# Projecting v in one matmul per tile with both weight parts side by side, and turning the row maxima with one matmul into 16 masked rows

## The reference

```python
# block 1: attention over the 1024 positions of an image, projections of width 32
q = einsum('mc,bcn->bmn', wq, x); k = ...wk...; v = ...wv...
att = softmax(einsum('bmi,bmj->bij', k, q), axis=2)
x = x + einsum('cm,bmn->bcn', wo, einsum('bij,bmj->bmi', att, v))
# block 2: tokens (1024 x 64 per image)
t = to_tokens(x)
u = layernorm(t);  t = t + softmax(u @ u.T) @ u
# block 3: 8 experts, the best 2 of each token
t = t + top2_mixture_of_experts(layernorm(t))
out = from_tokens(t)
```

## Time and profile before

| What | us |
|---|---|
| Median of 3 runs (237.2 to 237.84) | 237.38 |
| Time of the profiled execution | 236.11 |
| Its span, from first to last instruction | 234.4 |
| PE busy | 205.7 |
| DVE busy | 151.6 |
| ACT busy | 109.6 |
| POOL busy | 72.8 |

### The profile page before, as it was taken

The page is one execution under the profiler, slowest core; times in us unless marked ns, Lnnn a source line. Parts: engine busy times, 40 slices in busy tenths (PEclk is TensorE's granted clock), DMA queues, the critical chain, the costliest instruction groups (busy, mean ns, idle before and its releaser), DMA issues.

```text
span 234.4 us, 2786 instructions
## 1 busy us (share of the span) xinstructions
PE 205.7 (88%) x987; PEld 102.5 (44%) x987; DVE 151.6 (65%) x364; ACT 109.6 (47%) x170; POOL 72.8 (31%) x88
## 2 busy tenths in 40 slices
PE   6899899989997889899799999999999996682494
PEld 1545343735342435445345443543533433261382
DVE  2789666578159546846886787486835467999070
ACT  3533545575954552685345337664546751110101
POOL 8140000070403000110213577003776300874940
PEclk9999999999999999999999999999999999998578
DMA  3770000000000000000000000100000200000022
GB/s 101 137 166 15 3 0 0 0 1 3 1 0 0 3 0 0 0 0 3 0 1 0 3 1 9 35 0 3 0 0 0 49 0 0 0 0 0 0 48 45
DMA packets 3341, 3.67 MB, mean 16 GB/s; under 512 B 2176, under 2 KB 2432, under 8 KB 3328
## 3 DMA queue, kind: packets, MB, share of 16 engines
q1 hardware_dynamic: 3328, 3.50, 6.9%
HBM read 2.45 MB, written 1.05 MB: 15 GB/s over the span
## 4 chain that ended last, share of the span: by engine, by line
PE 62%; DVE 22%; ACT 6%; POOL 3%; issue 3%; DMA 1%; SPq 1%; DVEq 0%; POOLq 0%
PE acc L498 24%; DVE rowmax L1064 7%; PE ring L559 6%; PE ring L491 5%; PE ring L560 5%; PE ring L473 4%; PE ring L601 3%; PE ring L602 2%; DVE prod L1205 2%; DVE qst L1056 2%; DVE stats L1097 1%; ACT prob L870 1%; PE ring L535 1%; PE ring L462 1%; PE ring L583 1%
## 5 line engine op out<-in xcount | busy, mean ns | idle before, releaser
L873 ACT ACTIVATE prob<-ring,shift 128x1024 f32<-128x1024 f32 x32 | 35.6, 1113 | 36.6 <-PE ring L560 36.5
L1064 DVE TENSOR_REDUCE rowmax<-ring 128x1 f32<-128x1024 f32 x32 | 37.7, 1218 | 11.4 <-PE ring L473 11.3
L373 POOL TENSOR_TENSOR sm<-sm,minus_half 128x8 f32<-128x8 f32 x8 | 15.8, 1974 | 83.6 <-DVE sm L1107 83.6
L870 ACT ACTIVATE prob<-ring 128x1024 f32<-128x1024 f32 x32 | 32.0, 1026 | 16.7 <-PE ring L491 16.6
L498 PE MATMUL acc<-prob,val 128*64 128x512 f32 x128 | 31.1, 605 | 1.0 <-ACT prob L870 1.0
L498 PE MATMUL acc<-prob,u 128*64 128x512 f32 x128 | 31.2, 606 | 0.3 <-ACT prob L873 0.3
L559 PE MATMUL ring<-zst 128*128 128x512 f16 x64 | 24.5, 384 | 3.8 <-DVE rowmax L1064 2.7
L1205 DVE TENSOR_TENSOR prod<-ring,gate 128x1024 f32<-128x1024 f32 x16 | 19.3, 1219 | 12.0 <-PE ring L602 12.0
L473 PE MATMUL ring<-qst,kst 96*128 96x512 f32 x64 | 22.4, 436 | 2.3 <-DVE kst L1061 1.0
L560 PE MATMUL ring<-zsw,zst 128*128 128x512 f16 x64 | 24.3, 379 | 0.0
L491 PE MATMUL ring<-kst,qst 98*128 98x512 f32 x64 | 20.8, 423 | 3.0 <-DVE kst L1077 1.2
(11 more groups left out here) (152 smaller groups left out, 316.1 us busy)
## 6 DMA issues: line engine op xcount, KB each, us to landing
xin<-in_x SPq DMA_DIRECT2D x8, 256.0 KB, 4.0
out<-ob SPq DMA_DIRECT2D x6, 128.0 KB, 2.3
e_in<-in_L_ffn_expert_w SPq DMA_DIRECT2D x2, 128.0 KB
out<-ob SPq DMA_DIRECT2D x4, 64.0 KB, 2.0
eb_in<-in_L_ffn_expert_b SPq DMA_DIRECT2D x8, 2.0 KB
wo<-in_L_conv_wo SPq DMA_DIRECT2D x2, 8.0 KB, 2.2
r_in<-in_L_ffn_router_w SPq DMA_DIRECT2D x2, 2.0 KB
w<-in_L_conv_wq SPq DMA_DIRECT2D x1, 16.0 KB, 3.2
```

The costliest lines, as they stand in the source:

```text
L373: pool.tensor_tensor(sm[:, 3, :], sm[:, 2, :], minus_half[:, :], ALU.pow).then_inc(s_rs, 1)
L870: act.activation(prob1[:, j % DEEP, :], flat(filled(act, f"st{j}", b)), ACT.Exp).then_inc(s_p1, 1)
L873: act.activation(prob2[:, j % DEEP, :], flat(filled(act, f"s{j}", b)), ACT.Exp, bias=shift[:, :], accum_out=rsum2[b % 2][:, j:j + 1]).then ...
L1064: dve.tensor_reduce(rowmax[:, tile:tile + 1], flat(filled(dve, f"mx{tile}", b)), AX.X, ALU.max).then_inc(s_mx, 1)
```

## The change

**v and x.** The two weight tensors become one, `vx` of 128 columns: 32 for the high part of v's weights, 64 for x, 32 for the rest of v's weights. PE issues one matmul of 128 columns for each tile in place of two of 96. The two parts of v now lie side by side, so ACT copies the first into `vpart` and DVE adds the second to it (a new function `values` on DVE, a TENSOR_TENSOR of 128 x 256). The buffer is released by this DVE instruction (`s_v`), no longer by ACT.

**The maxima.** `nmax` holds the 8 high parts and the 8 rests of a position in 16 neighbouring columns, and one matmul turns them into 16 rows of 128. A DVE instruction (16 x 1024) spreads them: row r of `kst` gets its 128 numbers repeated 8 times, times a mask (`own_tile`) that is one only in the columns of its own tile. The second scores take 112 rows in place of 98, with 16 rows of ones in `qst`. ACT has no part in it any more.

```diff
@@ project_v @@
-                    o = (tile % 4) * (M + C)
-                    pe.matmul(buf[:, tile // 4, o:o + M + C], toks, vx1[:, :], start=True, stop=False)
-                    mm = pe.matmul(buf[:, tile // 4, o:o + M + C], toks, vx2[:, :], start=False, stop=True)
+                    o = (tile % 4) * P
+                    mm = pe.matmul(buf[:, tile // 4, o:o + P], toks, vx[:, :], start=True, stop=True)
@@ max_row on PE @@
-                for tile in range(T):
-                    c = col(tile)
-                    mm = pe.matmul(flat(buf)[0:ROW + 2, c:c + P], nmax[:, tile, :], ident_r[:, :], start=True, stop=True)
-                mm.then_inc(s_fill, 1)
+                pe.matmul(buf[0:ROW + 2 * T, 0, 0:P], nmax[:, :], ident_r[:, :], start=True, stop=True).then_inc(s_fill, 1)
@@ scores1 @@
-                    pe.wait_ge(s_mrow, 2 * (b + 1))
+                    pe.wait_ge(s_mrow, b + 1)
-                    mm = pe.matmul(buf[:, h, :], qst[home][0:ROW + 2, col(j):col(j) + P],
-                                   kst[home][0:ROW + 2, h * CHUNK:(h + 1) * CHUNK], start=True, stop=True)
+                    mm = pe.matmul(buf[:, h, :], qst[home][0:ROW + 2 * T, col(j):col(j) + P],
+                                   kst[home][0:ROW + 2 * T, h * CHUNK:(h + 1) * CHUNK], start=True, stop=True)
@@ release @@
-            table = {"w3": (s_wts, 3), "q": (s_qs, b + 2), "k": (s_ks, b + 2), "vx": (s_vx, 2 * b + 2),
-                     "mr": (s_mrow, 2 * b + 2), "po": (s_po, b + 1), "uT": (s_z, 2 * b + 2),
+            table = {"w3": (s_wts, 3), "q": (s_qs, b + 2), "k": (s_ks, b + 2), "vx": (s_v, b + 1),
+                     "mr": (s_mrow, b + 1), "po": (s_po, b + 1), "uT": (s_z, 2 * b + 2),
@@ ACT @@
-                act.activation(val[b % 2][:, :, 0:M].rearrange("p (a t) c -> p a t c", a=2), b4[:, :, :, 0:M],
-                               ACT.Copy).then_inc(s_vx, 1)
+                act.activation(vpart[:, :, :].rearrange("p (a t) c -> p a t c", a=2), b4[:, :, :, 0:M],
+                               ACT.Copy)
-            def max_row(b):
-                buf = filled(act, "mr", b)
-                act.activation(kst[b % 2][ROW:ROW + 2, 0:CHUNK], buf[ROW:ROW + 2, 0, :], ACT.Copy).then_inc(s_mrow, 1)
@@ DVE @@
+            def values(b):
+                buf, _ = PLACE[("vx", b)]
+                dve.wait_ge(s_vx, b + 1)
+                b4 = ring[:, buf].rearrange("p a (t c) -> p a t c", c=P)
+                dve.tensor_tensor(val[b % 2][:, :, 0:M].rearrange("p (a t) c -> p a t c", a=2), b4[:, :, :, M + C:P],
+                                  vpart[:, :, :].rearrange("p (a t) c -> p a t c", a=2), ALU.add).then_inc(s_v, 1)
             def max_row(b):
                 buf = filled(dve, "mr", b)
-                dve.tensor_copy(kst[b % 2][ROW:ROW + 2, CHUNK:N], buf[ROW:ROW + 2, 1, :]).then_inc(s_mrow, 1)
+                rows = slice(ROW, ROW + 2 * T)
+                shape = [2 * T, 2, T // 2, P]
+                mask = own_tile[rows, :].rearrange("r (g h) -> r h g", h=2)
+                dve.tensor_tensor(kst[b % 2][rows, :].rearrange("r (h g n) -> r h g n", h=2, n=P),
+                                  buf[rows, 0, 0:P].unsqueeze(1).unsqueeze(1).to_broadcast(shape),
+                                  mask.unsqueeze(3).to_broadcast(shape), ALU.mult).then_inc(s_mrow, 1)
@@ set-up on DVE @@
+            dve.tensor_tensor(own_tile[ROW:ROW + 2 * T, :], ident[ROW:ROW + 2 * T, ROW:ROW + T],
+                              ident[ROW:ROW + 2 * T, ROW + T:ROW + 2 * T], ALU.add)
-            dve.memset(vx2[:, M:M + C].bitcast(F32), 0.0)
```

More of the change, by code:

```diff
@@ L113, in build @@
         w2 = sb("w2", [P, 2, 3, M], F32R)
-        vx1 = sb("vx1", [P, M + C], F32R)
-        vx2 = sb("vx2", [P, M + C], F32R)
+        vx = sb("vx", [P, M + C + M], F32R)
         wo_blk = sb("wo_blk", [P, 2, C + 1])
@@ L145, in build @@
         rowmax = sb("rowmax", [P, T])
-        nmax = sb("nmax", [P, T, ROW + 2], F32R)
+        nmax = sb("nmax", [P, ROW + 2 * T], F32R)
+        own_tile = sb("own_tile", [P, T])
+        vpart = sb("vpart", [P, T, M])
         prob1 = sb("prob1", [P, DEEP, N])
@@ L210, in build @@
         s_ks = sem("k_split")
-        s_vx = sem("v_and_x_ready")
+        s_vx = sem("v_part_and_x_ready")
+        s_v = sem("v_ready")
         s_mx = sem("rowmax_ready")
@@ L346, in _ @@
                                pattern=[[-1, P]], channel_multiplier=1).then_inc(s_const, 1)
-            pool.memset(nmax[:, :, :].bitcast(F32), 0.0)
+            pool.memset(nmax[:, :].bitcast(F32), 0.0)
             for home in range(2):
@@ L351, in _ @@
             pool.wait_ge(s_pool, 3)
-            pool.memset(qst[0][ROW:ROW + 2, :].bitcast(F32), 1.0).then_inc(s_pool, 1)
+            pool.memset(qst[0][ROW:ROW + 2 * T, :].bitcast(F32), 1.0).then_inc(s_pool, 1)
             pool.wait_ge(s_pool, 4)
-            pool.memset(qst[1][ROW:ROW + 2, :].bitcast(F32), 1.0).then_inc(s_const, 1)
+            pool.memset(qst[1][ROW:ROW + 2 * T, :].bitcast(F32), 1.0).then_inc(s_const, 1)
             pool.wait_ge(s_const, 3)
@@ L503, in weigh1 @@
             def weigh1(b, j):
+                if j == 0:
+                    pe.wait_ge(s_v, b + 1)
                 if j == 0 and b:
@@ L928, in _ @@
                 act.activation(w1[:, :, r, :], buf[:, 0, 0:2 * M].rearrange("p (a m) -> p a m", a=2), ACT.Copy).then_inc(s_wr1, 1)
-            act.activation(vx1[:, 0:M], buf[:, 0, 2 * M:3 * M], ACT.Copy).then_inc(s_wr1, 1)
+            act.activation(vx[:, 0:M], buf[:, 0, 2 * M:3 * M], ACT.Copy).then_inc(s_wr1, 1)
             for name, dst, s_rounded in (("q", qst[0], s_qr), ("k", kst[0], s_kr)):
@@ L942, in _ @@
             round_k(1)
-            max_row(0)
             for j in range(4):
@@ L953, in _ @@
             values(1)
-            max_row(1)
             round_x(2)
@@ L1067, in negate_max @@
                 dve.wait_ge(s_mx, T * (b + 1))
-                hi = nmax[:, :, ROW:ROW + 1]
-                rm = rowmax[:, :].unsqueeze(2)
+                hi = nmax[:, ROW:ROW + T]
+                rm = rowmax[:, :]
                 dve.tensor_scalar(hi, rm, -1.0, None, ALU.mult).then_inc(s_nm, 1)
                 dve.wait_ge(s_nm, 2 * b + 1)
-                dve.scalar_tensor_tensor(out=nmax[:, :, ROW + 1:ROW + 2], in0=rm, scalar=-1.0, in1=hi.bitcast(F32),
+                dve.scalar_tensor_tensor(out=nmax[:, ROW + T:ROW + 2 * T], in0=rm, scalar=-1.0, in1=hi.bitcast(F32),
                                          op0=ALU.mult, op1=ALU.subtract).then_inc(s_nm, 1)
@@ L1088, in tokens1 @@
                 dve.wait_ge(s_po, b + 1)
-                dve.wait_ge(s_vx, 2 * b + 2)
+                dve.wait_ge(s_vx, b + 1)
                 dve.tensor_tensor(tok1[b % 2][:, :, :], tdiv[:, :, :], xt[b % 2][:, :, :], ALU.add).then_inc(s_tk1, 1)
@@ L1223, in _ @@
                               .to_broadcast([P, 2, 3, M]), w1[:, :, :, :].bitcast(F32), ALU.subtract).then_inc(s_wts, 1)
-            dve.memset(vx2[:, M:M + C].bitcast(F32), 0.0)
-            dve.tensor_tensor(vx2[:, 0:M], buf[:, 0, 2 * M:3 * M], vx1[:, 0:M].bitcast(F32), ALU.subtract).then_inc(s_wts, 1)
+            dve.tensor_tensor(vx[:, M + C:P], buf[:, 0, 2 * M:3 * M], vx[:, 0:M].bitcast(F32), ALU.subtract).then_inc(s_wts, 1)
             split_x0(1)
@@ L1234, in _ @@
                     dve.tensor_tensor(lo, ring[rows, k, h, :], lo.bitcast(F32), ALU.subtract).then_inc(s_split, 1)
-            for tile in range(T):
+            row_max(0, 0)
+            dve.wait_ge(s_const, 3)
+            values(0)
+            for tile in range(1, T):
                 row_max(0, tile)
@@ L1249, in _ @@
             negate_max(1)
+            values(1)
             dve.tensor_copy(ident_h[:, :], ident[:, :])
@@ L1257, in _ @@
             split_k(2)
+            values(2)
             dve.wait_ge(s_er, 2)
@@ L1281, in _ @@
             negate_max(2)
+            values(3)
             max_row(2)
```

5 lines of the change are left out of this document (2 added, 3 removed).

## The result

| | Before | After |
|---|---|---|
| Median, us (4 runs each, side by side) | 237.29 (237.08 to 237.84) | 240.79 (239.76 to 241.14) |
| Ratio, 95% interval | | 1.0129 [1.0103, 1.0155] |
| Profiled execution, us | 236.11 | 239.76 |
| Its span, us | 234.4 | 238.0 |
| Its mean granted TensorE clock | 0.974 | 0.960 |

The forecast was 236.6 us with a range up to 238.1. The last two rows of the table already point at what is missing from it: PE worked at a lower clock.

What follows compares the result with a forecast made beforehand. PE was taken as the bound in most places (62% of the chain), with hand-overs over DVE deciding at others. The terms summed to -0.76 us, giving 236.6 us against the median of 237.38, range 235.4 to 238.1.

Steps and rivals of the forecast that it cites:

- The terms of the sum: Image 0 +0.90, image 1 +0.16, image 2's v -0.64, image 3's v with image 2's maxima -1.01, image 3's maxima -0.10, start -0.07.
- PE waits for the spread at images 0 and 1: Ahead of the second scores: the spread adds 0.52 us at image 0; st0 of image 1 starts 0.38 later.
- taken: 0.114: Distance in us between starts of the new v matmuls, so each image's v costs PE 0.91 us less.
- 0.64 forecast: Image 2's v, inside image 1's scores: st6 waits for DVE, so 0.64 of PE's 0.91 us come through.
- The first exponential of image 1: Held by other ACT work before, it would follow st0 directly and start only 0.16 us later than before.
- V's 0.91 us less on PE buys nothing there: Image 0, first maxima tile: PE already waited 0.16 us for DVE's last split of k; image 0's term is +0.90.
- The 1.01 us that the prediction took off there: Image 3's v and image 2's maxima: DVE waited 2.57 us for PE, so st0 comes 1.01 us sooner.
- what could prove it wrong: A PE clock fall in the new 1.4 us pause before image 0's third maxima tile, for which it had no price.
- The spread was not dear: Rival: the spread costs more than 1.22 us, each extra d costing 4d, 238.2 us with d = 0.4; chance 0.14.
- DVE did not wait for POOL: Rival: `values(0)` is held until POOL's pass over x ends, +1.5, so 238.1 us; chance 0.06.
- v's matmuls gave back what they should: Rival: v matmuls start 0.2 us apart, an image's v gives back 0.22 us, total 237.7 us; chance 0.05.
- image 2's v gave its share: Rival: image 2's v gives nothing, as DVE is late to `values(2)` or st6 waits: -0.12, 237.3 us; chance 0.20.

Runs made afterwards that it cites:

- e8: The changed kernel unaltered, measured again beside e6 and e7 on one chip: 240.33 us (4 runs), ratio to before 1.0111.
- e7: The changed kernel with 6 more filler matmuls (read by nobody), in image 2's pauses only: 238.97 us (4 runs), ratio to before 0.9971.
- e14: As e13, with five more fillers in the pause ahead of image 1's second scores: 234.74 us (6 runs), ratio to before 0.9878.
- e13: As e1, with two more fillers before the first projections: 236.46 us (4 runs), ratio to before 0.99.
- e15: The same kernel as e13, measured again beside e14 on one chip: 236.78 us (11 runs), ratio to before 0.9957.
- e6: The changed kernel with 10 more filler matmuls, in image 0's pauses only: 238.56 us (4 runs).
- e5: The kernel before, without its 3 + 3 fillers around the turning of image 0's maxima: 239.91 us (10 runs), ratio to before 1.0048.
- e1: The changed kernel with 16 more fillers, in pauses of images 0 and 2: 237.29 us (10 runs), ratio to before 1.001.
- e11: The kernel before with the v part alone, fillers in pauses of images 0 and 2, two more at the start: 233.70 us (4 runs), ratio 0.9833.
- e3: The kernel before with the maxima part alone, v as before: 240.42 us (10 runs); ratio 0.9974 without six slow runs.
- e10: The kernel before with 2 more fillers ahead of image 0's second scores and 6 in image 2's pauses: 236.04 us (6 runs), ratio 0.9949.

## Why the prediction was wrong

**The terms of the sum held.** In the fourth column of the table of stretches, where the clock stays up, each is within 0.1 us of its forecast and their sum is -0.70 against -0.69. The mechanisms did too: PE waits for the spread at images 0 and 1; v's matmuls stand (46.42 - 45.48) / 8 = 0.117 us apart (taken: 0.114); DVE was not late to `values(2)`, and st6 of image 1 came 2.85 us after its old place when v of image 2 was 3.56 late, so 0.71 of the 0.91 us came through (0.64 forecast). The first exponential of image 1 started 0.74 us after st0 (50.22 - 49.48), held by nothing else, as said.

**The step that failed** is the one that took PE's waits as free. "V's 0.91 us less on PE buys nothing there", said the prediction of image 0, and let PE "wait for the spread" at image 1. It put the cost of both at nothing beyond the wait. Behind these two pauses, which the change lengthened from 0.43 to 1.56 us and from none to 1.85, the clock fell in two of the three traces of the whole change without added fillers in the first (after and e8, not e7), and in five of the seven without fillers in the second. The other fall in the trace of after, behind the unchanged pauses of image 2, is partly chance: the trace of e8 does not have it. The 1.01 us that the prediction took off there did come (the stretch that holds them is 1.95 us shorter in e14, 1.87 forecast), but it took them off a profiled execution of before that had come through its old pauses without a fall. The prediction did name the clock as what could prove it wrong, but at one pause only (the one before image 0's third maxima tile, where it came true in one of four traces, e8, at 1.40 us), and gave it neither a price nor a chance.

The price in the traces is 1.58 and 1.62 us a fall in after and 1.44 in e13 (48.87 - 47.43); over all traces it is 1.24 (e15) to 1.66 (e6, 49.09 - 47.43), and 3.23 for the long one of e5. How many falls a run without a trace had can be roughly estimated from its mean clock: e14's best runs and the one such run of e15 have 0.978, and e15 with its one fall 0.971, so 0.007 a fall. It is rough because the end of the kernel counts as well (e14's profile has 0.974 without any fall before 208 us), and because not every fall costs the same: in e1 the runs at 0.957 took 237.2 and 237.4 us, those at 0.971 took 237.1. None of the eight runs of the changed kernel was above 0.960, and five of them had 0.945 or 0.946, four or five slow stretches below 0.978. That is what the trace of e8 (0.946) shows: 8 to 12, 14 to 19, 28 to 33 and 52 to 57 us, and the tail. The usual run of before, at 0.966 or 0.967, would have one or two by this estimate; no trace shows such a run. The profiled execution of after is the quickest of its four, and has two falls and a slow start.

**The rivals.** None of them was the case. The spread was not dear (1.23 us), v's matmuls gave back what they should, DVE did not wait for POOL (`values(0)` took 0.42 us at 14.70 while POOL worked from 14.12 to 16.47), and image 2's v gave its share. The one that made the kernel 1.3% slower, falls of the clock behind the waits, was missing from the list.

**What the two parts are worth at full clock** follows from e11 and e14. Up to st0 of image 3, counted from the first projection, e11 takes 129.87 us and e14 130.78; before took 131.48. So v in one matmul gives 1.6 us, and the maxima part, put on top of it, takes 0.9 back: two waits of PE for a spread that is 0.52 us longer than the copy (the stretches to st0 of images 0 and 1 are 0.52 and 0.54 us longer in e14 than in e11, the other two 0.06 and 0.08 shorter). The medians, 233.70 and 234.74 from different chips, say the same. The parts do not add up, for the maxima part alone costs nothing (e3, 127.24 us from the first maxima tile to st0 of image 3, as before). The difference lies mostly in the stretch to st0 of image 1: either part alone makes it shorter (by 0.19 us in e11, 0.14 in e3), both together longer (by 0.35 in e14). With v's part in, PE already waits 0.72 us for DVE there, so the time taken off its turning matmuls buys nothing and all of the longer spread comes on top. Best of all kernels here is e11, without the maxima part: 1.7% faster than before, and 1.0% faster than e10, before with fillers, on the same chip (233.70 and 236.04).

**What stays open.** Why one execution falls behind a pause and the next does not, at equal pauses (1.84 us in e7, 1.85 in e13). How often the kernel before falls at image 2, since only its quickest kind of run has a trace; e10's 0.5% speaks for some. The tail, too, is at 0.50 for some 7 to 10 us at a stretch between 213 and 232 in every profile, before's included, and in most for shorter stretches around it; its length differs from one to the next, and it was not filled. The Trainium skill (TensorE: Matmul & The Clock Gate, A second HAM failure mode: psum-queue depth-cycling) tells of a kernel whose clock went back and forth because PE idled briefly and often between groups of matmuls. The traces here agree in so far as single pauses of 1.56 and 1.85 us, in a kernel whose scores pass through three PSUM buffers in turn, stood ahead of falls; that it is the same behaviour is not shown.

## What to carry to other kernels

Where PE is both the bound and, at some places, waits for another engine, work taken off it there is not free: look at its busy time in the windows around each wait before and after, and count a fall of the clock with its price as a rival of its own. Before giving up such a change, put matmuls that nobody reads into the lengthened waits, as many as end before the wait does, and take several executions, since the falls come by chance and a single trace shows only some of the places. And measure a change of two parts as two, and together: here one part alone gave 1.6 us, the other alone 0.0, and both 0.7.

## What the runs showed of the hardware

- The granted clock fell to 1.2 GHz behind pauses of 1.10 us (e5, ahead of 25.25 us), 1.31 (e8, ahead of 15.29), 1.56 (after) and 1.85 us (e13), and in other traces did not fall behind equal ones. Ahead of the tail each fall cost 1.2 to 1.7 us, and a longer one 3.2 (e5).
- A kernel with more matmuls was faster: 16 more took 3 us off (e1 against e8, of different chips; ratios to before 1.001 and 1.0111), five more took 2.0 us off (e14 against e15, of one chip).
- Matmuls of float32 data with 128 weight columns start 0.114 us apart with 96 moving columns and 0.117 apart with 128, at full clock. With 98 weight columns and 128 moving ones it is 0.088: among these three the distance went with the weights, not with the moving columns. With 96 weight columns and 512 moving ones it is 0.24 (before, 8.82 and 9.06 us), so this holds for few moving columns only.
- At the start of after, the clock column read 1.00 while matmuls of 512 columns stood 0.42 us apart, against 0.24 in before.
